# A graph network's transition from the scan over x2 to the edge records: factors and carried parts in PSUM, not in SBUF

## What is computed

```python
x = _layernorm(x + _L0_gnn_ref(x, edge_attr_48, src, dst, L0_gnn_eps), axis=-1)
x = _layernorm(x + _L1_gnn_ref(x, src, dst, L1_gnn_W, L1_gnn_b), axis=-1)
x = _layernorm(x + _L2_gnn_ref(x, edge_index, L2_gnn_W, L2_gnn_b), axis=-1)
x = _layernorm(x + _L3_gnn_ref(x, edge_index, edge_attr_40, edge_weight, node_type_119, node_vec, batch0, ...), axis=-1)
```

```python
deg = jnp.bincount(row, length=n).astype(x.dtype)
norm = deg_inv_sqrt[row] * deg_inv_sqrt[col]
msg = norm[:, None] * x[col]
agg = jax.ops.segment_sum(msg, row, num_segments=n)
return jax.nn.relu(agg @ W.T + b)
```

## Time and profile before

| | |
|---|---|
| median of 3 runs | 3162.78 us |
| the three runs | 3155.09, 3162.78, 3171.98 us |
| the profiled execution, its own time | 3144.17 us |
| its span, first to last instruction | 3142.4 us |
| DVE busy | 1940.1 us, 62% |
| POOL busy | 1776.5 us, 57% |
| ACT busy | 643.1 us, 20% |
| PE busy | 615.5 us, 20% |

### The profile page before, as it was taken

How to read it: one execution, slowest core, us unless ns; L and a number is a source line. 1 busy time by engine, 2 the same in 40 slices (tenths; PEclk the granted TensorE clock), 3 DMA queues, 4 the chain that set the end, 5 groups by cost and what they waited for, 6 DMA issues and landing times.

```text
span 3142.4 us, 12819 instructions
## 1 busy us (share of the span) xinstructions
PE 615.5 (20%) x2850; PEld 488.1 (16%) x2850; DVE 1940.1 (62%) x2769; ACT 643.1 (20%) x1141; POOL 1776.5 (57%) x1768
## 2 busy tenths in 40 slices
PE   1112500000277544554331000011023000000000
PEld 0000200000266444443331000010023000000000
DVE  2001899988776546655538289930026999998863
ACT  1002600221233222111111223310001113232110
POOL 5773004774555553765677776677723305564776
PEclk8555855555565555665555555555555555555555
DMA  3110194885134223221000444421111112220000
GB/s 115 22 21 10 48 331 165 314 295 213 30 119 147 94 89 101 65 57 31 14 17 20 170 118 141 142 76 29 19 33 34 67 57 80 82 75 26 17 17 14
DMA packets 110179, 276.20 MB, mean 88 GB/s; under 512 B 38521, under 2 KB 63427, under 8 KB 109971
## 3 DMA queue, kind: packets, MB, share of 16 engines
q1 hardware_dynamic: 46371, 196.46, 17.3%
q0 software_dynamic: 56448, 44.23, 7.5%
q10 hardware_dynamic: 7280, 34.67, 3.0%
HBM read 142.41 MB, written 138.17 MB: 89 GB/s over the span
## 4 chain that ended last, share of the span: by engine, by line
DVE 38%; issue 26%; another core or an unknown queue 16%; ACT 7%; PE 7%; POOL 5%; DMA 1%; SPq 0%; DVEq 0%; ACTq 0%; POOLq 0%
PE PS L930 4%; DVE PS L1382 3%; DVE var L1391 3%; POOL x_table L519 3%; DVE du L1385 3%; PE PS L916 2%; POOL ring L462 2%; DVE sumb L1308 2%; ACT sq L610 1%; DVE do L1402 1%; ACT GX L667 1%; DVE do L1151 1%; DVE MG L1375 1%; DVE GX L1404 1%
## 5 line engine op out<-in xcount | busy, mean ns | idle before, releaser
L505 POOL DMA_INDIRECT ring<-h_by_src,zs x196 | 206.6, 1054 | 330.5 <-ACTq L851 179.8
L475 POOL DMA_INDIRECT XD<-xa_table,dstI x196 | 187.7, 958 | 289.5 <-SPq L370 230.1
L462 POOL DMA_INDIRECT ring<-x_with_degree,srcI x196 | 208.2, 1062 | 149.4 <-DVEq L1466 87.8
L519 POOL DMA_INDIRECT x_with_degree<-sumb,put x196 | 195.7, 998 | 169.8 <-ACTq L691 113.4
L610 ACT ACTIVATE sq<-du 128x1344 f32<-128x1344 f32 x128 | 167.7, 1321 | 561.8 <-DVE du L1385 437.4
L519 POOL DMA_INDIRECT x_table<-sumb,put x196 | 214.1, 1093 | 90.6 <-issue 59.4
L519 POOL DMA_INDIRECT out<-sumb,put x196 | 195.1, 996 | 98.4 <-issue 60.9
L475 POOL DMA_INDIRECT XD<-in_xaux,srcI x196 | 188.9, 964 | 85.8 <-issue 59.5
L462 POOL DMA_INDIRECT ring<-edge_records,dstI x196 | 187.5, 957 | 84.7 <-issue 58.6
L1278 DVE TENSOR_SCALAR GX<-GX 128x784 bf16<-128x784 int16 x196 | 75.0, 428 | 252.8 <-remote 211.1
L475 POOL DMA_INDIRECT XD<-x_table,srcI x196 | 192.3, 981 | 59.8 <-issue 59.8
(11 more groups left out here) (295 smaller groups left out, 2668.9 us busy)
## 6 DMA issues: line engine op xcount, KB each, us to landing
din<-in_xaux SPq DMA_DIRECT2D x56, 728.0 KB
xa_table<-din SPq DMA_DIRECT2D x28, 728.0 KB
x_table<-GX SPq DMA_DIRECT2D x28, 686.0 KB
x_with_degree<-GX SPq DMA_DIRECT2D x28, 686.0 KB
din<-x_table SPq DMA_DIRECT2D x28, 686.0 KB
x_table<-do SPq DMA_DIRECT2D x28, 672.0 KB
din<-x_table SPq DMA_DIRECT2D x28, 672.0 KB
out<-do SPq DMA_DIRECT2D x28, 672.0 KB
```

The source lines that it names most:

```text
L462: pool.indirect_dma_start(ring[:, h, t, 0:w], None, table, bass.IndirectOffsetOnAxis(ap=of[:, c * H + t:c * H + t + 1], axis=0), **skip).t ...
L475: pool.indirect_dma_start(XD[:, t, 0:w], None, table, bass.IndirectOffsetOnAxis(ap=of[:, t:t + 1], axis=0)).then_inc(rows[c].sem, rows[c]. ...
L505: pool.indirect_dma_start(ring4[:, c % 4, t, :], None, H2, bass.IndirectOffsetOnAxis(ap=of[:, c * H + t:c * H + t + 1], axis=0), bounds_ch ...
L519: pool.indirect_dma_start(table, bass.IndirectOffsetOnAxis(ap=put[:, c * H + t:c * H + t + 1], axis=0), rows_of[:, h, t, :], None, bounds_ ...
```

## The change

The factor row of the last rows is first copied to PSUM (`t0P`) and the large product reads it there. The factor row of the 48 scans is written to `t0P` as well, and not to `t0`. The suffix's `carried` gets a half of `factorP` for its work tile, the two halves in turns.

```diff
-            one(V.tensor_tensor(M, XS[:, :, :], along(end[:, :]), ALU.mult))
-
-            one(V.tensor_scalar(t0[:, :], end[:, :], -1.0, 1.0, ALU.mult, ALU.add))
+            one(V.tensor_copy(t0P, end[:, :]))
+            one(V.tensor_tensor(M, XS[:, :, :], along(t0P), ALU.mult))
+
+            one(V.tensor_scalar(t0P, end[:, :], -1.0, 1.0, ALU.mult, ALU.add))
             for f in range(D):
-                V.tensor_tensor_scan(M[:, ::-1, f], t0[:, ::-1], M[:, ::-1, f], 0.0, ALU.mult, ALU.add
+                V.tensor_tensor_scan(M[:, ::-1, f], t0P[:, ::-1], M[:, ::-1, f], 0.0, ALU.mult, ALU.add
                     ).then_inc(own.sem, own.add())
...
             for i in range(NBLK):
-                carried(bass.ds(i * R, R), suf)
+                carried(bass.ds(i * R, R), suf, work=factorP[:, i % 2, :, :])
                 dve.sem_inc(S["rec_ready"], 1)
```

## The result

The changed kernel takes 3177.23 us (median, 3162.54 to 3211.76), the kernel before, beside it on the same chip, 3158.89 us. The ratio is 1.0064, 95% interval 1.0039 to 1.0089: **0.6% slower**, some 20 us, where 0.35% faster was forecast. The profiled execution took 3165.31 us.

The account below looks back on a forecast made before the run. POOL's last x2 scatter turn was taken to end the stage: 16.4 us freed on POOL, less 5.4 us of new waiting for ACT, gives 11.0 us, so 3162.8 - 11.0 = 3151.8 us, 0.35% faster; range 3140 to 3163 us.

Parts of the forecast that it names:

- What bounds the kernel now: x2 scatter stage: POOL's last turn ends it; POOL's scatters are stretched beside DVE instructions reading two SBUF tensors.
- Rival B: Scatters beside product and suffix: any long DVE instruction stalls POOL, so nothing is gained, 3162.8 us; chance 0.13.
- Parts 1, 2, 3 and 5: DVE's copy 0.40 us, product unchanged at 9.96 us, one-minus-end row +0.10 us, suffix product into PSUM zero.
- Part 4: The 48 scans with their factor in PSUM: zero change, or 4.3 us if their back-to-back overlap is lost.
- the sum for DVE: DVE reaches its first block of carried parts about 0.5 us later, bounds 0 to 5 us.
- What is late next: ACT's record pieces and last staging hold POOL's last turn: POOL waits 5.4 us, the turn starts 11.0 us earlier.
- Rival A: ACT's record pieces run faster and do not hold back POOL's last turn: full 16.4 us gained, 3146.4 us; chance 0.12.
- Rival C: The 48 PSUM scans lose overlap and more; gain gone at 0.23 us each, 3173.9 us at double pace; chance 0.07.
- The chance of 0.04 for slower: Whole kernel: probability given to being slower by over 0.5%, which needs 3178.6 us.
- The stages behind it moved by 11 us without change: After the x2 scatters: later stages start 11 us earlier and give none of it back.

Follow-up runs that it names:

- e1: Changed kernel, but the large product reads its factor from SBUF again, without the copy before it; scans and suffix stay in PSUM: 3186.1 us, ratio 1.0002.
- g1: Kernel before, with POOL's x2 gather paced: turn c, from 2 on, waits for c - 1 blocks of h2: 3022.24 us, ratio 0.9473.
- g2: Kernel before, with POOL's x2 gather paced: turn c, from 2 on, waits for c blocks of h2: 3034.81 us, ratio 0.9518.
- f5: Changed kernel, product cut in two; POOL waits after turn 9's fifth scatter for the first part: one run, 3165.31 us (before 3162.51).
- the run h2: Changed kernel, with POOL holding turn 9's first scatter until DVE reaches the copy ahead of the product: one run, 3128.05 us (before 3156.55).
- e3: Kernel before, with only the suffix's work tile moved to PSUM; product and scans in SBUF: 3186.88 us, ratio 1.0016.
- f1: Changed kernel, with POOL waiting after turn 9's fifth scatter until DVE's product is done: one run, 3170.45 us (before 3162.51).
- h3: The kernel of f5, timed against the kernel before: 3138.83 us, ratio 0.995.
- g4: Changed kernel, with the suffix's carried parts cut into 14 halves instead of 7 blocks: one run, 3211.56 us (before 3188.4).

## Why the prediction was wrong

**What bounds the kernel now: right, but the reading stopped short.** The stretched scatters of the earlier trace rows were the two-SBUF instructions, and they vanished: 0.97 us beside the product, 16.4 us less in the group. Rival B is out. The Trainium skill (SBUF — State Buffer, section "Who interferes with whom") infers that a `tensor_tensor` leaves descriptor generation alone. The traces disagree: 10.38 to 10.47 us beside the product from two SBUF tensors in the kernel before, e1, g1 and g2, and 0.97 us with one of them in PSUM. Its other rule, contention with two SBUF inputs, agrees.

**Parts 1, 2, 3 and 5: right.** The copy 0.37 us (0.40 taken), the product 9.96 us, the one-minus-end 0.37 us, L1374 into PSUM 1.56 us.

**Part 4 and the sum for DVE: the step that failed.** "DVE is thus about 0.5 us later at its first corrected block (bounds 0 to 5 us)" was measured as 28.1 us, and 0.4 us for the copy. A scan by itself costs what I said, 0.46 us from start to start, and e1 shows that for all 48. The error was to bound DVE's cost by DVE's own instructions only. The removed stall of POOL was a cost to POOL and at the same time the break that kept DVE's and TensorE's short instructions quick. Rows that would have warned me were in the trace of the kernel before. In the h2 stage three engines are idle for 27 to 44 us at a time, `<-issue` and `<-remote`, beside an unbroken row on POOL. And 53 us into the row that begins at 1258.90, instructions of DVE that had followed each other every 0.26 us start 0.70 us and more apart:

```profile
1312.01 0.34 DVE L1522 SCALAR_TENSOR_TENSOR sq<-iotaz,zd,PS 128x120 f32<-128x120 bf16 x1 [0.70 <-issue]
```

I had not asked why, since these stages were not touched.

**What is late next: right in kind, wrong in who.** "Each microsecond that DVE is slower before its first block goes straight off the gain" is what happened. The first record piece starts 66.2 us behind the product's start instead of the 38.1 us that the forecast comes to (1717.95 - 1679.41 - 0.4, both kernels counted from their products). That is 28.0 us, the loss on DVE. POOL's wait before the last turn was 33.14 us and not 5.4 us. Its last turn started 99.34 us behind the product and not 71.95 us (1751.76 - 1679.41 - 0.4): 27.4 us, the 28.0 less 0.6 us by which the 14 pieces ran quicker (32.15 against 32.76 us). Where the loss is taken away, this part of the forecast comes out, size and path: in f5 the pieces start 38.3 us behind the product, ACT's last staging starts 32.8 us later, POOL waits for it by 1.16 us on top of its own pause of 5.09 us, and its last turn starts at +72.17 us. The stage gains 101.2 - 90.1 = 11.1 us, and 11.4 us in the run h2, for the 11.0 us of the forecast. **Rival A** is out: from the first piece to the last staging are 32.6 to 32.9 us in e1, e3, f1, f5 and the run h2, against 32.76 us before.

**Rival C** had the right place, engine and sign. The scans took 12.8 us more, 0.27 us each, just over its 0.23 us at which the gain is gone; the other 15.2 us of the loss lie behind the scans, where it had nothing. Its mechanism, PSUM scans that lose their overlap, is refuted by e1 and by the run h2. The chance of 0.04 for slower was too small, since I had given it to this mechanism only.

**"The stages behind it moved by 11 us without change"** could not be shown in the changed kernel. In e1, e3, f1, f5 and h3, whose stage is 5 to 11 us shorter, the gather of records takes 276.4 to 276.8 us instead of 271.9 us: 4.7 us are given back there, at POOL's waits for the dense pairs. So e1 and e3, with 7.1 and 5.5 us gained in the stage, keep 2.4 and 0.6 us, too little to measure. Why those waits lengthen was not looked into; g2, whose stage is as long as before, has 276.0 us as well, so the shorter stage is not the whole reason.

**What stays open.** The experiments show that POOL's unbroken row is what costs the 28 us here, and that a break takes the slow steps away. They do not show the mechanism in the chip: what the engines lack while `<-issue` stands ahead of their instructions, why steps are multiples of 0.70 us, or what decides when they begin. Neither time nor the number of DMAs since the last break does it alone: the slow steps came after 16 us in g1, 51 us in the changed kernel, 149 us in the row from 505.32 us, and in the row of 148 us not at all. The length of the shortest break that helps is not known either: 5.09 us sufficed ahead of the scans, in g1 waits of 3.25 us and more ended them, and a gather of 2.08 us at 2169.52 us in the kernel before, held for 1.1 us, did not. The traces come from profiled executions, and the timed ones agree with them in size (h3, g1); whether the profiler has a part in the state itself can't be told from these runs.

## What to carry to other kernels

A stall that is removed may have been a pause that something else needed: when a producer of long rows of indirect DMAs becomes quicker, look at what the other engines do beside the row, from its first tens of us to its end. Read idle time marked `<-issue` or `<-remote` between short instructions beside such a row as a cost of the row, not of these engines, even where the stage is not part of the change. Such a row does not always have this cost: the same handoffs beside 112 scatters in 148 us had none. Where POOL has slack behind it, let it wait for the others' progress every few turns: a few waits of 3 to 12 us here were worth 5% of the kernel.

## What the hardware showed that was not expected

- Beside an unbroken row of indirect DMAs on POOL (0.97 us each, 0.30 us between), scans of 0.57 us start 1.40 us apart instead of 0.46 us, in the changed kernel from about 51 us into the row on, and the steps behind them wait 1.25 to 9.27 us instead of at most 0.6 us. Beside the x2 gather a block of h2 takes 117.6 us instead of 14.6 us.
- It does not come beside every such row: none beside 112 scatters in 148.4 us or 99 scatters in 128.9 us of the kernel before, and after 16 us of a row already in g1.
- The last slow step comes 7.4 us after the row's end in g4, and in the kernel before 27 us after the end of the gather (DVE's L1691 at 2331.73, after 3.74 us `<-remote`, against 2304.57).
- A scan with its factor in PSUM costs the same as from SBUF, 0.46 us start to start, also back to back, and a scatter beside it takes 0.97 us instead of 1.07 us.
- A scatter that starts beside a DVE product of two SBUF tensors is held until the product is done, 10.4 us for 9408 elements a partition; with one operand in PSUM it is not held at all.
